# A decoder layer with 16 experts on one core: rows scattered from where x2 stays, top four taken from the logits, and the orders of the cross attention rebuilt five rounds deep

## What is computed

```python
x = layernorm(x + attn(x))                        # one head of 256, softmax over 1024 keys
x = layernorm(x + xattn(x, ctx, mask, causal))    # this is x2; 16 heads of 16, 64 keys
logits = x @ router_w + router_b
probs  = softmax(logits)                          # 16 experts
topw, topi = top_k(probs, 4);  topw = topw / sum(topw)
combine = sum(one_hot(topi) * topw)               # the share of each expert in each row
out = sum_e (gelu(x @ w1[e] + b1[e]) @ w2[e] + b2[e]) * combine[:, e]
return layernorm(x + out)
```

## Time and profile before

| | us |
|---|---|
| runs | 634.44, 634.78, 635.58; median 634.78 |
| the profiled execution | 640.26 |
| its span | 638.3 |
| self attention and setup, up to the first scores of the cross attention | about 171 |
| cross attention with router, up to the last carry | about 140 |
| shares, bias sums and table, up to the first turn of expert rows | 23 |
| expert loop | about 275 |
| last sums and norm | about 29 |

### The profile page before, as it was taken

One profiled execution on the slowest core, in us unless ns is written; L12 is line 12 of the kernel. 1 busy time (PEld: TensorE's weight loads), 2 busy tenths in 40 slices (PEclk: granted clock), 3 DMA queues, 4 the chain that ended last, 5 costly groups with the idle time before them and its releaser, 6 DMA issues.

```text
span 638.3 us, 14320 instructions
## 1 busy us (share of the span) xinstructions
PE 550.0 (86%) x4060; PEld 514.3 (81%) x4060; DVE 429.9 (67%) x1061; ACT 342.7 (54%) x627; POOL 288.2 (45%) x262
## 2 busy tenths in 40 slices
PE   6999999999789999985499899999999999899700
PEld 5978888888679988875368899999899999899700
DVE  2645555555357888885546788878787888778326
ACT  2433333333135666663307677777777777677504
POOL 5541111111101466666610466656766666567623
PEclk9999999999769999998558999999999999999955
DMA  8899999400000122212275988899999999989477
GB/s 278 306 398 396 398 396 396 140 0 1 0 1 2 44 76 83 79 70 87 100 277 182 248 233 243 228 231 243 254 249 248 227 249 247 238 229 245 51 183 237
DMA packets 91675, 124.37 MB, mean 195 GB/s; under 512 B 6624, under 2 KB 62832, under 8 KB 91648
## 3 DMA queue, kind: packets, MB, share of 16 engines
q1 hardware_dynamic: 73984, 102.31, 48.3%
q0 software_dynamic: 14592, 19.41, 15.8%
q10 hardware_dynamic: 3072, 2.33, 1.1%
HBM read 61.88 MB, written 62.14 MB: 194 GB/s over the span
## 4 chain that ended last, share of the span: by engine, by line
PE 44%; DMA 17%; issue 14%; DVE 13%; SPq 5%; ACT 4%; POOL 2%; DVEq 1%; ACTq 0%; POOLq 0%
PE ps L348 9%; PE ps L350 8%; PE ps L349 8%; DMA w1f<-in_L_ffn_w 8%; DMA xg<-expert_rows 3%; DVE w_l L1457 3%; DMA expert_sum<-yb,home_row 2%; PE ps L885 2%; PE ps L730 2%; DMA expert_rows<-xd,idx 2%; PE ps L819 2%; PE ps L793 2%; PE ps L803 2%; DVE w_h L1450 2%; SPq L393 1%
## 5 line engine op out<-in xcount | busy, mean ns | idle before, releaser
L564 POOL DMA_INDIRECT expert_sum<-yb,home_row x80 | 165.5, 2068 | 123.3 <-DVE home_row L1485 100.6
L348 PE MATMUL ps<-gT_h,w_h 128*128 128x256 f32 x320 | 95.2, 297 | 1.8 <-issue 1.3
L348 PE MATMUL ps<-w_h,h_h 128*128 128x256 f32 x320 | 90.8, 284 | 2.0 <-DVE h_l L1478 2.0
L349 PE MATMUL ps<-gT_l,w_h 128*128 128x256 f32 x320 | 91.9, 287 | 0.0
L350 PE MATMUL ps<-gT_h,w_l 128*128 128x256 f32 x320 | 91.8, 287 | 0.0
L349 PE MATMUL ps<-w_l,h_h 128*128 128x256 f32 x320 | 90.5, 283 | 0.0
L350 PE MATMUL ps<-w_h,h_l 128*128 128x256 f32 x320 | 90.5, 283 | 0.0
L1095 ACT ACTIVATE hf<-ps,b1s 128x256 f32<-128x256 f32 x160 | 62.9, 480 | 31.9 <-PE ps L350 31.7
L545 POOL DMA_INDIRECT expert_rows<-xd,idx x64 | 62.8, 981 | 32.9 <-issue 21.1
L1478 DVE TENSOR_TENSOR h_l<-hf,h_h 128x1024 fp32r<-128x1024 f32 x40 | 49.0, 1225 | 32.9 <-ACT h_h L1102 32.3
L348 PEld LDWEIGHTS ps<-gT_h,w_h 128*128 128x128 f32 x320 | 62.5, 195 | 2.4 <-issue 1.5
(11 more groups left out here) (239 smaller groups left out, 1383.2 us busy)
## 6 DMA issues: line engine op xcount, KB each, us to landing
expert_rows<-zeros SPq DMA_DIRECT2D x32, 1088.0 KB, 13.7
w1f<-in_L_ffn_w SPq DMA_DIRECT2D x40, 512.0 KB, 5.9
w2f<-in_L_ffn_w SPq DMA_DIRECT2D x40, 512.0 KB, 4.2
xg<-expert_rows SPq DMA_DIRECT2D x40, 272.0 KB, 4.3
total<-expert_sum SPq DMA_DIRECT2D x16, 256.0 KB, 6.2
expert_sum<-zeros SPq DMA_DIRECT2D x1, 2304.0 KB, 15.9
x_all<-in_x SPq DMA_DIRECT2D x8, 256.0 KB, 7.0
expert_sum<-x_all ACTq DMA_DIRECT2D x8, 256.0 KB, 5.1
```

Source lines behind the costliest of these rows:

```text
L348: pe.matmul(o, ah, bh, start=first, stop=False)
L349: pe.matmul(o, ah, bl, start=False, stop=False)
L564: pool.indirect_dma_start(out=sums[p], out_offset=bass.IndirectOffsetOnAxis(ap=home_row[:, p, c:c + 1], axis=0), in_=yb[:, p, c], in_offse ...
```

## The change

**x2 stays where it is.** `x_all` gets rows of 288 values: x2, the 16 shares, the home row, and padding. The shares are written into it, the home row once at the start. POOL scatters four times from that one tile. The buffer `xd`, `pack`, the two operations that filled its last columns, and the waits on landed scatters are gone. `idx` has a place for each tile. The expert rows in DRAM, their zeroing and the loads in the expert loop are 288 values wide.

**Top four from the logits.** The largest eight are taken of the logits. ACT negates the first of them (neg_max), takes the exponentials of all 16 (rexps, without a sum), and those of the top four with their sum (top_sum). DVE inverts this sum and forms all shares. The maximum, the division of all 16 and the sum of four are gone from the DVE.

**The expert loop.** DVE copies 17 values of a row where it was two. ACT reads the step's expert from the table with a register load in each step (y_out), and takes that expert's share as its scale.

**Orders and banks.** The deepest skew is 5, which makes 21 rounds. Positions go to bank 6, the turned x2 to bank 7. POOL's rounds are all written out, with root2 between the third and the fourth scatter. x2 plus the bias sums goes to `ot`, and from there to DRAM.

```diff
-RW = D + 16
+RW = D + 2 * E
+HOME = D + E
-        x_all = sb("x_all", [P, NT, D])
-        shares = sb("shares", [P, NT, E])
+        x_all = sb("x_all", [P, NT, RW])
+        idx = sb("idx", [P, NT, K], U32)
...
-        idx = sbe("idx", [P, 2, K], U32)
-        xd = sbe("xd", [P, 2, K, RW])
...
+            def send(t, p, k, r):
+                pool.indirect_dma_start(
+                    out=xg_dram, out_offset=bass.IndirectOffsetOnAxis(ap=idx[:, t, r:r + 1], axis=0),
+                    in_=x_all[:, p * TPB + k], in_offset=None).then_inc(sc_dma[p][r], 16)
             def dispatch(t, p, k):
                 pool.wait_ge(lidx, done(t))
-                pool.wait_ge(dest, done(t))
-                pool.wait_ge(lw, done(t))
-                pool.wait_ge(xdc, done(t))
+                pool.wait_ge(lsh, done(t))
+                pool.wait_ge(x2k, done(t))
...
+                for r in range(K - 1):
+                    send(t, p, k, r)
+            def dispatch_last(t, p, k):
+                send(t, p, k, K - 1)
-            pipeline(pool, NT, [(1, causal), (3, root2), (6, dispatch)])
+            for t in range(NT + 5):
+                for skew, fn in [(1, causal), (5, dispatch), (3, root2), (5, dispatch_last)]:
...
-            pipeline(pe, NT, [(1, cscores), (3, turn_o), (4, turn_x2), (2, cturn_p), (6, positions), (3, project),
-                              (0, cquery), (4, logits), (2, cattend)])
+            pipeline(pe, NT, [(1, cscores), (4, logits), (3, turn_o), (2, cturn_p), (3, project), (0, cquery),
+                              (2, cattend), (4, positions), (3, turn_x2)])
...
-            def pack(t, p, k):
-                act.wait_ge(x2k, done(t))
-                if not (isinstance(t, int) and t < 2):
-                    for r in range(K):
-                        act.wait_ge(sc_dma[p][r], 16 * k)
-                act.sem_inc(passed, 1)
-                act.activation(xd[:, p, :, 0:D], x_all[:, ds(p * TPB + k, 1), :].broadcast_to([P, K, D]), ACT.Copy).then_inc(xdc, 1)
+            def neg_max(t, p, k):
+                act.wait_ge(l8, done(t))
+                act.activation(lmax[:, p:p + 1], mx8[:, p, 0:1], ACT.Copy, scale=-1.0).then_inc(lmx, 1)
+            def top_sum(t, p, k):
+                act.wait_ge(lwi, freed(t))
+                act.activation(top[:, p], mx8[:, p, 0:K], ACT.Exp, bias=lmax[:, p:p + 1], accum_out=wsum[:, p:p + 1]).then_inc(lws, 1)
...
-                     ramp=[(3, o_out), (4, x2_turned), (2, p_out), (0, q_out), (1, cexps), (5, pack), (4, keep_x2), (4, rexps)], ramp_steps=RAMP)
+            pipeline(act, NT, [(4, x2_turned), (4, keep_x2), (3, o_out), (2, p_out), (4, neg_max), (4, rexps), (1, cexps), (4, top_sum), (0, q_out)])
...
             def y_out(t, p, k):
                 act.wait_ge(yps, done(t))
                 act.wait_ge(hmon, done(t))
+                expert = act.value_load(tab[1:2, ds(t, 1)], min_val=0, max_val=E - 1)
...
-                    ins = act.activation(yb[:, p, c], ps[:, 6 + p, c * D:(c + 1) * D], ACT.Copy, scale=home_on[:, p, c, 1:2])
+                    ins = act.activation(yb[:, p, c], ps[:, 6 + p, c * D:(c + 1) * D], ACT.Copy, scale=home_on[:, p, c, ds(expert, 1)])
...
-                dve.max(mx8[:, p], rp[:, p]).then_inc(l8, 1)
+                dve.max(mx8[:, p], lg[:, p]).then_inc(l8, 1)
...
-            pipeline(dve, NT, [(5, router_inv), (1, head_max), (5, router_probs), (1, sub_max), (5, largest), (3, residual2),
-                               (5, chosen), (3, stats2), (5, chosen_float), (6, rows_of), (3, aggr2), (6, next_rows), (5, one_hot),
-                               (3, var2), (6, pick_rows), (5, chosen_mask), (6, slots), (5, all_shares), (6, indices),
-                               (3, norm2), (2, head_inv), (2, head_norm), (4, logits_out), (4, logits_max)])
+            pipeline(dve, NT, [(3, head_inv), (5, rows_of), (3, head_norm), (5, next_rows), (5, pick_rows), (5, slots), (5, indices),
+                               (1, head_max), (4, logits_out), (4, largest), (1, sub_max), (3, residual2), (4, chosen), (3, stats2),
+                               (4, chosen_float), (3, aggr2), (4, one_hot), (3, var2), (4, chosen_mask), (4, share_sum), (4, all_shares),
+                               (3, norm2)])
...
-                dve.tensor_copy(home[:, p], xg[:, p, :, D:D + 2]).then_inc(hm, 1)
+                dve.tensor_copy(home[:, p], xg[:, p, :, D:HOME + 1]).then_inc(hm, 1)
```

More of the change, by code:

```diff
@@ L221, in decoder_layer @@
         lexp = sbe("lexp", [P, 2, E])
-        lsum = sbe("lsum", [P, 2])
-        linv = sbe("linv", [P, 2])
-        rp = sbe("rp", [P, 2, E])
+        top = sbe("top", [P, 2, K])
         mx8 = sbe("mx8", [P, 2, 8])
@@ L759, in cquery_of @@
                 pe.wait_ge(cqc, freed(t) + 1)
-                if not (isinstance(t, int) and t < 4):
-                    pe.wait_ge(x2t, done(t - 4))
                 for oc in range(KD):
@@ L799, in cattend @@
                 pe.wait_ge(co, freed(t) + 1)
-                if not (isinstance(t, int) and t < 3):
-                    pe.wait_ge(lgb, done(t - 3))
+                if not (isinstance(t, int) and t < 2):
+                    pe.wait_ge(lgb, done(t - 2))
                 for g, pair in enumerate(SCORED):
@@ L808, in turn_o @@
                 pe.wait_ge(coc, freed(t) + 1)
+                if not (isinstance(t, int) and t < 2):
+                    pe.wait_ge(lcar, done(t - 2))
                 for kc in range(KD):
@@ L815, in project @@
                 pe.wait_ge(cres, freed(t) + 1)
-                if not (isinstance(t, int) and t < 4):
-                    pe.wait_ge(lcar, done(t - 4))
+                pe.wait_ge(x2t, freed(t) + 1)
                 for kc in range(KD):
@@ L873, in _ @@
                 for t in range(4 * g, 4 * g + 4):
-                    mm = pe.transpose(ps[0:E, g % 2, (t % 4) * P:(t % 4 + 1) * P], shares[:, t], ident[:])
+                    mm = pe.transpose(ps[0:E, g % 2, (t % 4) * P:(t % 4 + 1) * P], x_all[:, t, D:D + E], ident[:])
                 mm.then_inc(sh_pe, 1)
@@ L1034, in x2_turned @@
                 act.wait_ge(lg_ps, freed(t))
-                act.activation(x2T[:, p].rearrange("p k c -> p (k c)"), ps[:, 4, D:2 * D], ACT.Copy).then_inc(x2t, 1)
+                act.activation(x2T[:, p].rearrange("p k c -> p (k c)"), ps[:, 7, D:2 * D], ACT.Copy).then_inc(x2t, 1)
             def keep_x2(t, p, k):
                 act.wait_ge(x2, done(t))
-                act.activation(x_all[:, ds(p * TPB + k, 1), :], xs[:, ds(p, 1), :], ACT.Copy).then_inc(x2k, 1)
-            def pack(t, p, k):
-                act.wait_ge(x2k, done(t))
-                if not (isinstance(t, int) and t < 2):
-                    for r in range(K):
-                        act.wait_ge(sc_dma[p][r], 16 * k)
-                act.sem_inc(passed, 1)
-                act.activation(xd[:, p, :, 0:D], x_all[:, ds(p * TPB + k, 1), :].broadcast_to([P, K, D]), ACT.Copy).then_inc(xdc, 1)
+                act.activation(x_all[:, ds(p * TPB + k, 1), 0:D], xs[:, ds(p, 1), :], ACT.Copy).then_inc(x2k, 1)
+            def neg_max(t, p, k):
+                act.wait_ge(l8, done(t))
+                act.activation(lmax[:, p:p + 1], mx8[:, p, 0:1], ACT.Copy, scale=-1.0).then_inc(lmx, 1)
             def rexps(t, p, k):
                 act.wait_ge(lmx, done(t))
-                act.activation(lexp[:, p], lg[:, p], ACT.Exp, bias=lmax[:, p:p + 1], accum_out=lsum[:, p:p + 1]).then_inc(lex, 1)
-            pipeline(act, NT, [(3, o_out), (4, x2_turned), (2, p_out), (1, cexps), (0, q_out), (5, pack), (4, keep_x2), (4, rexps)],
-                     ramp=[(3, o_out), (4, x2_turned), (2, p_out), (0, q_out), (1, cexps), (5, pack), (4, keep_x2), (4, rexps)], ramp_steps=RAMP)
+                act.wait_ge(lsh, freed(t))
+                act.activation(lexp[:, p], lg[:, p], ACT.Exp, bias=lmax[:, p:p + 1]).then_inc(lex, 1)
+            def top_sum(t, p, k):
+                act.wait_ge(lwi, freed(t))
+                act.activation(top[:, p], mx8[:, p, 0:K], ACT.Exp, bias=lmax[:, p:p + 1], accum_out=wsum[:, p:p + 1]).then_inc(lws, 1)
+            pipeline(act, NT, [(4, x2_turned), (4, keep_x2), (3, o_out), (2, p_out), (4, neg_max), (4, rexps), (1, cexps), (4, top_sum), (0, q_out)])
             act.dma_start(b1r[:], b1).then_inc(ld_c, 16)
```

94 lines of the change are left out of this document (38 added, 56 removed).

## The result

On one chip the changed kernel took 641.12 us (median of 18 executions, 634.37 to 647.16) against 635.53 for the kernel before (18 executions, 628.49 to 641.39). The ratio is **1.0078, 95% interval 1.0046 to 1.0109: slower**, where I had forecast 629.3 us. Single executions of either kernel spread over 2%, and part of what follows is why.

The account below looks back on a forecast made before the run. It took the ring of index, scatters, landing, pack and exponentials, 14.44 us over two rounds, to bound the cross attention; 2.9 - 1.1 - 7.9 - 1.9 + 2.5 = -5.5 off the median 634.78 gave 629.3 us, range 623.5 to 636.

Parts of the forecast that it names:

- Ramp, +2.9: Start to the scores of tile 3: later copies on ACT make it 2.9 us longer (0 to +4.1).
- Steady rounds, -1.1: Scores of tile 3 to tile 15: twelve rounds of 6.95 us, 83.4 in all, 1.1 less.
- my second rival: Steady rounds: the new rings replace the old one, rounds back at 7.22, +2.1 for -1.1, 632.5 us; chance 0.13.
- one through POOL: Steady rounds: norm2, DVE operations to the index, three scatters, root, back to norm2, 6.88 us.
- My ring through ACT: Steady rounds: norm2, turn of x2, scores, logits, probabilities, exponentials, sum, shares, back to norm2, about 6.9 us.
- the rival in which scatters and DVE meet: Steady rounds: scatters stretch to 1239 ns, POOL's ring grows by 0.83 us, +4.5, 639.3 us; chance 0.04.
- Tail, -7.9: Tile 15's scores to the last carry: 25.0 us for 32.9, no DMA wait after the last norm (-6.9 to -8.9).
- Carry to expert rows, -1.9: Last carry to first turned expert rows: the 1.90 us hole between the halves of the shares closes (-1.5 to -1.9).
- sums and loads of xg cover them: Carry to expert rows: bias sums and loads of xg (4 us) hide POOL's eight last scatters, ending near 312.
- Expert loop, +2.5: Expert loop: wider rows, longer DVE copies and ACT's register load add 2.5 us (0 to +6).
- the rival in which ACT becomes the bound: Expert loop: the register load makes ACT the bound, 10 us at 0.25 a step, 638.8 us; chance 0.13.
- PE's old floor: Cross attention rounds: PE's own work from scores to scores without a gap, 6.89 us.

Follow-up runs that it names:

- a_again: The changed kernel profiled once more, nothing changed: 637.81 us.
- two_two: Kernel of x2_ramp_b, but two scatters ahead of the root and two behind norm2's end, for three and one: 627.5 us, 0.992 of the kernel before.
- late_ramp: Changed kernel, fourth scatter waiting for the next round's context product, ACT's old order in the first three rounds: 631.32 us, 0.995 of the kernel before.
- b_again: The kernel before profiled once more, nothing changed: 643.91 us.
- x2_ramp_b: Changed kernel, fourth scatter waiting for norm2's end, ACT's old order in the first three rounds, on the chip of after_b: 625.72 us, 0.9856 of the kernel before.
- after_b: The changed kernel again, unaltered, on another chip: 632.81 us, 0.9986 of the kernel before.
- ramp_b: Changed kernel with ACT's old order in the first three rounds alone, on the chip of after_b: 629.04 us, 0.9970 of the kernel before.
- no_load: Changed kernel without ACT's register load in the expert loop, a fixed column scaling the result (shares left out): 637.09 us.

## Why the prediction was wrong

*Ramp, +2.9.* Right in mechanism and size: +3.8 in the recorded pair, +1.4 in a_again. The terms I had bounded (0 to +4.1) hold.

*Steady rounds, -1.1: the step that failed.* I wrote "PE's products are the same, 6.89 a round" and took 6.95. Three things replaced it.
- The smooth round is 7.04 to 7.39, twelve of them 86.3. That is the time of my second rival (rounds back at 7.22), though not its ring. I had summed two rings, one through POOL and one through ACT, and left out the one that binds: norm2, turn of x2, the next scores, head_max, and DVE's run of work up to the next norm2, 7.14 or 7.32 us. My ring through ACT had its first steps (norm2, turn, scores) but went on to the logits. It costs 2.9 us against the 83.4 that I had.
- The collision. For the rival in which scatters and DVE meet I looked only at what DVE does to a scatter, "by the greatest row that costs at most 0.28", and gave it 0.04. The cost lies the other way: a scatter that begins inside norm2 can hold DVE's next operation until 0.3 to 0.6 us after its own end, and leaves a hole of 1.0 to 1.4 us (2.4 us in all in the steady rounds of the recorded execution outside the slow one). The Trainium skill, "SBUF — State Buffer", section on two separate sides, gives the shared ports for a whole instruction to whichever starts first, a GpSimd operation or a DVE operation in a two-port mode or with two SBUF inputs. By that rule head_inv, with one input in PSUM, need not wait for a scatter, and it did in 17 rounds. Nor do the scatters look as if they waited for norm2's end: of the 98 that began inside norm2 in seven executions, nearly all that began up to 0.14 us after its start took 1.04 us, as behind norm2, the later ones took 1.16 to 1.18, and both kinds are among the 17. I had read the rule in one direction only. The step I skipped is to ask, for the scatter I put behind the root, what DVE starts at that same moment: norm2, released by that very root.
- In the recorded execution one round had a mean clock of 0.68 and took 10.06 for 7.2, some 3 us. In the 10 us before the clock fell, at 253.1, PE was busy for 9.18; in two_two it was 9.80 before a round of the same kind. Such a round is also in kernels without any hole (late_ramp, two_two), in b_again, and not in x2_ramp_b. What brings it stays open.

Together, in the recorded execution: 86.3, plus 2.9 for the slow round, plus 2.4 for the holes in the others (8.10, 7.74 and 8.13 for 7.2), is 91.6, and 91.67 was measured. Before had 84.5 in its smooth execution and 93.7 in the other. How often each kernel is disturbed thus moves a single execution more than the change does; how much of the medians it makes is not shown.

*Tail, -7.9: right in kind, too large.* 30.3 for 25.0. The last norm to the carry was exact. I had 5.95 from the scores to norm2 of tile 13, and it took 9.19: a hole of 1.25 at 286.4 and a round with PE at 1.2 GHz. I had 6.85 for each of the last two rounds, and they took 7.97 and 7.86, because the ring of those rounds runs through PE's turns and the projection, and DVE waits 2.78 for it. I had put half clock into the positions alone. Where no hole of 1 us came the tail took 26.2 (after_b, mean clock 0.73) or 28.8 (ramp_b, 0.63), still 1.2 and 3.8 over my sum.

*Carry to expert rows, -1.9.* It came to -2.1, but that is no proof of the term: the kernel before took 21.5 itself in b_again, as the changed one does. The shares close up as foretold, and PE would be ready at 333.69 (338.37 less the wait of 4.68). But "sums and loads of xg cover them" fell in the recorded execution. DVE's table is done at 322.14 and PE's turn of it at 323.18, yet DVE copies it only at 325.44, after 3.30 us put down to "remote". Then come SP's register loads (from 325.76) and the load of xg, issued at 330.38. In a_again the wait ahead of the expert rows is 1.64, as it was before (1.53), and the stretch is 21.3 all the same.

*Expert loop, +2.5.* Wrong in sign by the two pairs: 299.0 and 300.1 for 302.2 and 303.9. no_load shows the register load to cost nothing measurable, so the rival in which ACT becomes the bound falls as well. Why the loop is about 3 us shorter was not tried; over all kernels with the new loop it took 296.8 to 302.3.

*The sum.* My forecast needed nothing disturbed and rounds at PE's old floor. after_b, with one round at a lower clock and no hole, came to 626.2 of span, yet the median even on that chip is that of the kernel before.

## What to carry to other kernels

When a GpSimd instruction is moved behind one that releases another engine, ask what that engine starts in the same moment; here one wait for the end of norm2, with the old order of three rounds, made of a kernel at 1.008 and 0.999 of the one before one at 0.989 and 0.986. When a list is put in a new order, follow the rings that close through every operation that now stands behind a wait: PE, busy for 42.71 of 43.37 us, was not the bound, but one link of a ring through norm2, the turn, the scores and DVE. And before a change of 1% is judged, look at two executions of each kernel round by round, since a few disturbed rounds outweigh the change.

## What the runs showed that I had not expected

A GpSimd scatter that started 0.10 to 0.16 us after a DVE operation from SBUF to SBUF (norm2) held up, in 17 cases, DVE's following operation, which reads only PSUM, by 1.0 to 1.4 us, until 0.31 to 0.57 us after the scatter's recorded end. In the 81 other rounds with a scatter begun inside norm2 nothing was held up for 0.6 us or more; what decides is open. Started 0.70 us behind norm2's start, it never did. Something like it is in the kernel before: in b_again its residual started, three times, about 1.1 us after the end of a scatter inside which it fell due.

In a trace PE can look busy throughout and still wait: with PE busy for 42.71 of 43.37 us, the turn of x2 started 0.06 us after norm2's end in every round.
